# Node_b of layers 2 and 3: split in SBUF and turned by DMA instead of by PE, in newly arranged periods

## The chip, the core and the metric

The kernel runs on one core of a Trainium2 chip. The metric is the device time of one execution in microseconds, median of several runs. Engines are named as in the profile: PE (matmuls), PEld (its weight loads), DVE (VectorE), ACT (ScalarE), POOL (GpSimd), SP (SyncE, which issues all DMAs here).

## What is computed

Sixty-four graphs of 128 nodes with 384 features each pass through four blocks, each one `x = x + f(relu(layernorm(x)), adj)`. The first block has two layers (0 and 1 in the kernel), the second two (2 and 3), the third and fourth one each (4 and 5). The second block's layer, in which the changed values live, is

```
h = relu(hidden)                       # node_b, 128 nodes x 384
m_left  = h @ W_left.T                 # and m_right = h @ W_right.T
u = triu(h m_left^T) + tril(h m_right^T) ; attn = softmax of u/sqrt(384) over the edges
out = attn @ (h @ W_lin.T + b_lin) ; layer norm ; next layer
```

Blocks 3 and 4 are attention with 12 heads under the adjacency matrix; block 3 ends in an output product (Wo), block 4 does not. All large products are made from f16 halves: a value v is held as hi = f16(v) and lo = f16(v - hi), and a product takes three matmuls (hi hi, lo hi, hi lo).

## The kernel before

PE needs the node features with the features on the partitions, so each layer begins with a turning: `node` (128 nodes x 384, f32, SBUF) becomes three 128x128 blocks in a PSUM bank by three matmuls with the identity (`turned`, L420), ACT takes the high half out of the bank with Relu, and DVE the low half. For layers 2 and 3 these are `turned(b0, node_b[l])`, `htb_hi` (ACT, L721) and `htb_lo` (DVE, L871, `relu_lo`). The probabilities of layers 4 and 5 go another way: they are split in SBUF (`prob_halves`, DVE L1079 and POOL L1220) and turned by one DMA transpose for each quad of heads (`pt_halves`, SP, L315), eight a graph.

Nothing is scheduled by a compiler. On each engine the work of a graph is written as several streams (Python generators), one step for each `yield`: on PE `a` and `w` (layers 0 and 1: chain and weight products), `b` and `x` (layers 2 and 3), `c`, `y` and `t` (layers 4 and 5). `woven` runs them in periods: the string `ORDER[engine]` says letter by letter whose next step comes, `FIRST` in which period and at which occurrence a stream begins. So in one period PE works on graph g in layers 0 and 1, on an older graph in layers 2 and 3 and on a still older one in layers 4 and 5. Each engine takes its instructions strictly in this order and waits on semaphores. `SPLITS` places the splitting of the 19 weights into halves (ACT high, DVE low, one weight each time) in the first periods, and `WARM_FIRST` and `WARM_LAST` put small matmuls on ones (L626, L630) into gaps of PE in the first and last periods.

Steps that the prediction speaks of, by tile and line:

- Layer 0 and 1 on PE: turning of node_a (L420), scores, the left, right and self products (weights 0 to 5, bank_a, L374, 128x384 matmuls: a first half of four and a rest of five), turning of attn_a (L457), context product `sides` x `attn_ta`. ACT's copy L714 scales the self product by d_sum from bank a0 to a1 and so frees a0, into which attn_a is turned.
- Layers 2 and 3 on PE: left product (L406 high groups, L413 low part), right product (nine matmuls for each of three column groups, L374), score product, turning of attn_b (L505), context product lin x attn_tb.
- Layer 4 to layer 5: Wo (L374 on bank_c), `x` updated by DVE (L1119), norm (DVE stats_c, mean_var_c, var_eps_c; POOL rstd_c; DVE shift_c L1129), `node_c` by ACT (L651), its turning on PE (L420 on bank_c).
- The buffer `pt_halves` is one for both layers: the transpose of quad j of layer 4 waits until the product of quad j of layer 5 (of the older graph, L579 to L581 on bank_a) has read it.

## Time and profile before

| | us |
|---|---|
| median of 3 runs | 2900.89 (2900.38 to 2901.71) |
| the profiled execution, device time | 2899.22 |
| its span, first to last instruction | 2897.5 |
| PE busy in the span | 2794.9 |
| DVE busy | 2424.7 |
| ACT busy | 2116.5 |
| POOL busy | 846.4 |

The page of the profile gives the span, the busy time of each engine and the costliest groups of instructions. The timeline gives start and length of each instruction, in us from the start of the span, with the idle time before it and its releaser in brackets. Matmuls are pipelined, so starts are to be compared, not ends: the time that a matmul takes from PE is the distance to the start of the next.

### The profile page before, as it was taken

What the parts mean: (1) busy time and instruction counts of PE and PEld (TensorE: products, weight loads), DVE (VectorE), ACT (ScalarE), POOL (GpSimd) and SP (SyncE); (2) the same over time, 40 slices, a digit from 0 to 9 for tenths busy, and PEclk for the clock granted to TensorE, in tenths of its full rate; (3) what the DMA queues carried; (4) which work ended last, traced back from release to release, by engine and by line L of the source; (5) the groups of instructions that cost most, each with busy time, mean ns of one, the idle gap of its engine ahead of it and who ended that gap; (6) DMA issues with size and microseconds to landing.
All of it is one profiled execution on the core that took longest, in us unless ns stands there. A gap on an engine that the chain in (4) does not pass through costs nothing.

```text
span 2897.5 us, 87504 instructions
## 1 busy us (share of the span) xinstructions
PE 2794.9 (96%) x33735; PEld 2130.6 (74%) x33735; DVE 2424.7 (84%) x7450; ACT 2116.5 (73%) x6036; POOL 846.4 (29%) x1227
## 2 busy tenths in 40 slices
PE   6999999999999999999999999999999999999998
PEld 4777777777777777777777777677777777777787
DVE  5788888888888888898888888888888888888884
ACT  5677777777777777777677777777777777777763
POOL 0133233233233233233232332232332332332331
PEclk8999999999999999999999999999999999999999
DMA  6132232232232232232232322322322222322222
GB/s 220 21 56 45 50 54 45 52 53 46 52 55 44 52 54 45 52 56 43 51 49 46 55 47 49 54 46 48 57 45 49 57 47 47 57 44 49 54 50 42
DMA packets 458222, 154.85 MB, mean 53 GB/s; under 512 B 415312, under 2 KB 457808, under 8 KB 457808
## 3 DMA queue, kind: packets, MB, share of 16 engines
q1 hardware_dynamic: 457808, 149.25, 27.2%
q8 instruction: 270, 4.42, 0.6%
q14 instruction: 144, 1.18, 0.1%
HBM read 35.92 MB, written 12.58 MB: 17 GB/s over the span
## 4 chain that ended last, share of the span: by engine, by line
PE 64%; DVE 17%; DMA 8%; issue 4%; POOL 4%; SPq 2%; ACT 1%; DVEq 0%; POOLq 0%; ACTq 0%
PE bank_c L374 23%; PE bank_a L374 13%; PE bank_b L374 13%; DMA pt_halves<-prob_halves 7%; PE bank_c L548 4%; DVE score L1064 4%; PE bank_b L406 3%; POOL prob_halves L1220 2%; DVE neg_head_max L1069 2%; PE bank_c L420 2%; SPq L315 2%; PE bank_b L413 1%; DVE scaled_b L995 1%; PE bank_b L420 1%; POOL rstd_c L1171 1%
## 5 line engine op out<-in xcount | busy, mean ns | idle before, releaser
L1220 POOL TENSOR_TENSOR prob_halves<-prob,prob_halves 128x384 f16<-128x384 f32 x512 | 473.7, 930 | 597.7 <-DVE prob_halves L1079 597.6
L785 ACT ACTIVATE prob<-score,neg_head_max 128x128 f32<-128x128 f32 x1536 | 494.8, 390 | 56.5 <-DVE neg_head_max L1069 54.6
L1064 DVE SCALAR_TENSOR_TENSOR score<-bank_c,bias 128x384 f32<-128x384 f32 x512 | 281.8, 550 | 212.8 <-PE bank_c L548 202.7
L374 PE MATMUL bank_c<-htc_hi,w_lo 128*128 128x128 f16 x2304 | 405.4, 219 | 0.0
L374 PE MATMUL bank_c<-htc_lo,w_hi 128*128 128x128 f16 x2304 | 405.4, 219 | 0.0
L374 PE MATMUL bank_c<-htc_hi,w_hi 128*128 128x128 f16 x2304 | 405.4, 219 | 0.0
L374 PE MATMUL bank_a<-w_hi,hta_hi 128*128 128x384 f16 x1152 | 375.4, 326 | 0.7
L374 PE MATMUL bank_a<-w_lo,hta_hi 128*128 128x384 f16 x1152 | 375.4, 326 | 0.0
L1069 DVE TENSOR_REDUCE neg_head_max<-score 128x3 f32<-128x384 f32 x512 | 280.0, 547 | 2.4
L374 PE MATMUL bank_a<-w_hi,hta_lo 128*128 128x384 f16 x1152 | 250.3, 326 | 0.0
L374 PEld LDWEIGHTS bank_c<-htc_lo,w_hi 128*128 128x128 f16 x2304 | 225.4, 98 | 13.8
L374 PEld LDWEIGHTS bank_c<-htc_hi,w_hi 128*128 128x128 f16 x2304 | 225.9, 98 | 12.3
L646 ACT ACTIVATE bank_a<-bias_rows 128x384 f32<-128x384 f32 x384 | 189.8, 494 | 61.3 <-DVE hta_lo L871 57.2
L374 PEld LDWEIGHTS bank_c<-htc_hi,w_lo 128*128 128x128 f16 x2304 | 225.4, 98 | 0.0
L374 PE MATMUL bank_b<-htb_hi,w_lo 128*128 128x128 f16 x1152 | 202.6, 219 | 0.0
L374 PE MATMUL bank_b<-htb_lo,w_hi 128*128 128x128 f16 x1152 | 202.5, 219 | 0.0
L374 PE MATMUL bank_b<-htb_hi,w_hi 128*128 128x128 f16 x1152 | 202.4, 219 | 0.0
L646 ACT ACTIVATE m_hi<-bank_b 128x384 f16<-128x384 f32 x256 | 124.0, 485 | 105.6 <-PE bank_b L413 60.9
L374 PE MATMUL bank_a<-sides,attn_ta 128*128 128x384 f32 x512 | 195.0, 503 | 0.0
L1171 POOL TENSOR_TENSOR rstd_bc<-var_eps_bc,minus_half 128x1 f32<-128x1 f32 x64 | 35.2, 551 | 529.3 <-DVE var_eps_bc L883 529.3
L374 PE MATMUL bank_c<-w_hi,htc_hi 128*128 128x384 f16 x576 | 188.7, 328 | 0.2
L374 PE MATMUL bank_c<-w_lo,htc_hi 128*128 128x384 f16 x576 | 187.9, 327 | 0.0
(202 smaller groups left out, 8991.2 us busy)
## 6 DMA issues: line engine op xcount, KB each, us to landing
x_in<-x SPq DMA_DIRECT2D x64, 192.0 KB, 2.4
out<-y_out SPq DMA_DIRECT2D x64, 192.0 KB, 2.4
pt_halves<-prob_halves SPq DMA_TRANSPOSE x512, 2.8
w_stage<-w_t SPq DMA_DIRECT2D x11, 576.0 KB, 5.7
adj_in<-adj SPq DMA_DIRECT2D x64, 64.0 KB, 2.1
adj_t<-adj_turned SPq DMA_DIRECT2D x64, 64.0 KB, 2.2
score<-w_t SPq DMA_DIRECT2D x4, 576.0 KB, 7.3
prob<-w_t SPq DMA_DIRECT2D x4, 576.0 KB, 7.5
```

What stands on the lines that cost most here:

```text
L315: sp.dma_start_transpose(pt_halves[:, j, :, :, :].rearrange("p h c n -> p (h c) n"), prob_halves[:, j, :, :, :].rearrange("p h c n -> p (h ...
L374: mm = nc.tensor.matmul(out_ap, a, b, start=first and i == 0, stop=last and i == len(pairs_of) - 1, skip_group_check=True)
L406: nc.tensor.matmul(bank[:, cols], w[:, m, c, cols], th[:, c, :], start=(o, c, n) == (0, 0, 0), stop=False, skip_group_check=True)
L413: mm = nc.tensor.matmul(bank[:, cols], w_hi[:, m, c, cols], tl[:, c, :], start=False, stop=(o, c) == (CHUNKS - 1, CHUNKS - 1), skip_group_ ...
L420: mm = nc.tensor.matmul(bank[:, c * 128:(c + 1) * 128], src(c), ident[:, :], start=c == 0, stop=True, is_transpose=True, skip_group_check= ...
L548: mm = nc.tensor.matmul(c_banks[j][:, c * 128:(c + 1) * 128], qk[rows, c, 0, :], qk[rows, c, 1, :], start=c == 0, stop=True, skip_group_ch ...
L646: return nc.scalar.activation(dst, src, ACT.Copy, scale=scale)
L785: ex = nc.scalar.activation(prob[:, j, c, :], score[:, j, c, :], ACT.Exp, bias=neg_head_max[:, j, c:c + 1])
L1064: V.scalar_tensor_tensor(score[:, j, :, :], chunked(c_banks[j][:, 0:D]), scale, bias[:, :].unsqueeze(1).to_broadcast([128, CHUNKS, 128]), ...
L1069: V.tensor_reduce(neg_head_max[:, j, :], score[:, j, :, :], AX.X, ALU.max, negate=True)\
L1171: P.tensor_tensor(rstd[of][:, :], src, exponent[:, :], ALU.pow).then_inc(root_ready[of][g], 1)
L1220: P.tensor_tensor(prob_halves[:, j, 1, :, :], prob[:, j, :, :], prob_halves[:, j, 0, :, :], ALU.subtract)\
```

## The change

Node_b is no longer turned by PE. ACT writes the high half of node_b (Relu, f16) into `node_b_halves` in SBUF, DVE the low half beside it, and SP turns both with one DMA transpose for each layer into `htb`, whose two halves are the former `htb_hi` and `htb_lo`. The step `turned(b0, node_b...)` is gone from PE's stream `b` (8 steps a graph become 6), SP gets a new stream `b` with two steps a graph. Node_b needs one buffer instead of two. The left product waits for the landing (`htb_landed`) instead of for each half. The wait for the former reader of bank b0 moves to the right product.

All tables of the order are new: the strings of all five engines (turned round, so that a period now begins about where place 21 of PE's string was before, and with steps exchanged), FIRST, the places of the weight splits and the warming matmuls.

```diff
-    "pe": "cwyybwwbwwcbyayyyyyyyxxcxxxxxabxtxyyyybyaybyaywwtbwwwwxxaxxccxxcxcacbaxcxccaw",
+    "pe": "xxcxxxxxabtxxyyyabyybayyywwtwwwwxaxxcxxcccxxacabxxcccawcwyybwbwwcwyyyyyyyya",
...
-    "sp": "lsttttttttu",
+    "sp": "lbtttbtttttsu",
...
-    "act": [(0, -1), (0, -1), (0, -1), (0, -1), (0, -1), (0, -1), (0, -1), (0, 24),
+    "act": [(0, 5), (0, 32), (0, 42), (0, 54), (0, 59), (1, 4), (1, 21), (1, 21),
...
-        node_b = ring("node_b", 2, [128, D])
-        htb_hi, htb_lo = sb("htb_hi", [128, CHUNKS, 128], f16), sb("htb_lo", [128, CHUNKS, 128], f16)
+        node_b = sb("node_b", [128, D])
+        node_b_halves, htb = (sb(n, [128, 2, CHUNKS, 128], f16) for n in ("node_b_halves", "htb"))
+        htb_hi, htb_lo = htb[:, 0, :, :], htb[:, 1, :, :]
...
+            def turn_nodes_b(g):
+                for k in (1, 2):
+                    sp.wait_ge(*htb_lo_ready.at(g, k))
+                    if k == 1 and g:
+                        sp.wait_ge(*lin_done.at(g - 1, 2))
+                        sp.wait_ge(*ub_done.at(g - 1, 2))
+                    sp.dma_start_transpose(htb[:, :, :, :].rearrange("p h c n -> p (h c) n"),
+                                           node_b_halves[:, :, :, :].rearrange("p h c n -> p (h c n)"))\
+                        .then_inc(htb_landed[g], 16)
+                    yield
...
-                    pe.wait_ge(*node_b_ready.at(g, k))
-                    if l == 0 and g:
-                        pe.wait_ge(*scaled_b_ready.at(g - 1, 2))
-                    turned(b0, lambda c: node_b[l][:, c * 128:(c + 1) * 128]).then_inc(tb_done[g], 1)
-                    yield
...
-                    pe.wait_ge(*htb_hi_ready.at(g, k))
+                    pe.wait_ge(*htb_landed.at(g, k))
...
-                    act.wait_ge(*tb_done.at(g, k))
-                    nc.scalar.activation(htb_hi[:, :, :], chunked(b0[:, 0:D]), ACT.Relu).then_inc(htb_hi_ready[g], 1)
+                    act.wait_ge(*node_b_ready.at(g, k))
+                    if l == 0 and g:
+                        act.wait_ge(*htb_landed.at(g - 1, 2))
+                    nc.scalar.activation(node_b_halves[:, 0, :, :], chunked(node_b[:, :]), ACT.Relu).then_inc(htb_hi_ready[g], 1)
...
-                    relu_lo(htb_lo[:, :, :], b0, htb_hi[:, :, :]).then_inc(htb_lo_ready[g], 1)
+                    node_lo(node_b_halves, node_b).then_inc(htb_lo_ready[g], 1)
```

How the order moved at three places. PE in steady state, around the turning of node_c for layer 5: `w_hi,hta_hi` and `w_lo,hta_hi` on bank_a are the self product of layer 0, `w_hi,hta_lo` its low part. Before:

```order
L374 MATMUL bank_a<-w_hi,hta_hi 128x384
L374 MATMUL bank_a<-w_lo,hta_hi 128x384
L374 MATMUL bank_a<-w_hi,hta_hi 128x384
L374 MATMUL bank_a<-w_lo,hta_hi 128x384
L374 MATMUL bank_a<-w_hi,hta_hi 128x384
L374 MATMUL bank_a<-w_lo,hta_hi 128x384
L374 MATMUL bank_a<-w_hi,hta_lo 128x384 x3
L420 MATMUL bank_c<-ident,node_c 128x128 x3
L420 MATMUL bank_b<-ident,node_b 128x128 x3
```

Now:

```order
L387 MATMUL bank_a<-w_hi,hta_hi 128x384
L387 MATMUL bank_a<-w_lo,hta_hi 128x384
L387 MATMUL bank_a<-w_hi,hta_hi 128x384
L387 MATMUL bank_a<-w_lo,hta_hi 128x384
L433 MATMUL bank_c<-ident,node_c 128x128 x3
L387 MATMUL bank_a<-w_hi,hta_hi 128x384
L387 MATMUL bank_a<-w_lo,hta_hi 128x384
L387 MATMUL bank_a<-w_hi,hta_lo 128x384 x3
```

The second half of the self product stood ahead of node_c and stands behind it; node_b's turning is gone.

DVE in steady state, from the attention of layer 3 (attn_b) to shift_c, with which ACT makes node_c of layer 5. `x_1<-bank_c,x_1` is the update by Wo. Before:

```order
L985 TENSOR_SCALAR attn_b<-delta_b,r_den_b 128x128
L1119 SCALAR_TENSOR_TENSOR x_1<-bank_c,x_1 128x384
L868 SCALAR_TENSOR_TENSOR attn_tb_lo<-bank_b,attn_tb_hi 128x128
L883 TENSOR_SCALAR var_eps_ab<-squares_ab 128x1
L874 BN_STATS stats_c<-x_1 128x6
L877 BN_AGGR mean_var_c<-stats_c 128x2
L1125 TENSOR_SCALAR var_eps_c<-mean_var_c 128x1
L907 SCALAR_TENSOR_TENSOR attn_a,edge_sum<-expo_a,adj_in 128x128
L887 TENSOR_TENSOR shift_ab<-neg_mean_ab,rstd_ab 128x1
L1129 SCALAR_TENSOR_TENSOR shift_c<-mean_var_c,rstd_c 128x1
L874 BN_STATS stats_b<-bank_b 128x6
```

Now (just ahead of these rows stand attn_b and the bias of layer 5, `bias<-adj_in,beta_col,no_edge`):

```order
L921 SCALAR_TENSOR_TENSOR attn_a,edge_sum<-expo_a,adj_in 128x128
L901 TENSOR_TENSOR shift_ab<-neg_mean_ab,rstd_ab 128x1
L925 SCALAR_TENSOR_TENSOR junk_a,d_sum<-attn_a,ident 128x128
L1133 SCALAR_TENSOR_TENSOR x_1<-bank_c,x_1 128x384
L878 SCALAR_TENSOR_TENSOR attn_tb_lo<-bank_b,attn_tb_hi 128x128
L888 BN_STATS stats_c<-x_1 128x6
L928 SCALAR_TENSOR_TENSOR den_a<-z_sum,edge_sum 128x1
L891 BN_AGGR mean_var_c<-stats_c 128x2
L1139 TENSOR_SCALAR var_eps_c<-mean_var_c 128x1
L888 BN_STATS stats_b<-bank_b 128x6
L891 BN_AGGR mean_var_b<-stats_b 128x2
L1143 SCALAR_TENSOR_TENSOR shift_c<-mean_var_c,rstd_c 128x1
```

The bias, attn_a, shift_ab and junk_a moved ahead of the update of x, and stats_b with its aggregate between var_eps_c and shift_c.

ACT at the start of the program: `w_hi` rows are weight splits, `spent_in` belongs to the input's norm of graph 0. Before:

```order
L848 ACTIVATE w_hi<-w_stage 128x1152 x2
L848 ACTIVATE w_hi<-score 128x1152
L848 ACTIVATE w_hi<-prob 128x1152
L848 ACTIVATE w_hi<-w_stage 128x1152 x2
L848 ACTIVATE w_hi<-score 128x1152
L656 ACTIVATE spent_in,total_in<-x_in 128x384
L646 ACTIVATE neg_mean_in<-total_in 128x1
L662 ACTIVATE spent_in,squares_in<-x_in,neg_mean_in 128x384
L848 ACTIVATE w_hi<-prob 128x1152
L848 ACTIVATE w_hi<-w_stage 128x1152
L651 ACTIVATE node_a<-x_in,shift_in,rstd_in 128x384
```

Now:

```order
L664 ACTIVATE spent_in,total_in<-x_in 128x384
L858 ACTIVATE w_hi<-w_stage 128x1152
L654 ACTIVATE neg_mean_in<-total_in 128x1
L670 ACTIVATE spent_in,squares_in<-x_in,neg_mean_in 128x384
L858 ACTIVATE w_hi<-w_stage 128x1152
L659 ACTIVATE node_a<-x_in,shift_in,rstd_in 128x384
L858 ACTIVATE w_hi<-score 128x1152
L703 ACTIVATE hta_hi<-bank_a 128x384
```

Two weight splits instead of nine stand ahead of node_a of graph 0. One more pair of rows moved on PE without a table here: the turning of attn_a of layer 1 (L457) stood behind twelve high matmuls of layer 3's left product and stands now behind six of them.

## Rows read from the trace of the kernel before

**Rows 1.** The page, part 1: busy us (share), instructions.
```profile
PE 2794.9 (96%) x33735; PEld 2130.6 (74%) x33735; DVE 2424.7 (84%) x7450; ACT 2116.5 (73%) x6036; POOL 846.4 (29%) x1227
```

**Rows 2.** Windows by stage: from:to us, then busy by engine, clock, DMA share, GB/s.
```profile
0.00:30.00 30.00, 8.83 (x118) 8.66 (x118) 12.16 (x18) 13.55 (x16) 2.39 (x12) 0.71 0.94 333
30.00:62.30 32.30, 27.49 (x269) 20.40 (x269) 20.09 (x42) 20.10 (x37) 1.65 (x3) 0.95 0.46 155
...
171.10:2783.90 2612.80, 2550.80 (x30600) 1934.27 (x30599) 2241.26 (x6959) 1957.53 (x5633) 790.88 (x1139) 1.00 0.27 50
2783.90:2897.50 113.60, 101.12 (x1592) 87.98 (x1590) 66.87 (x171) 49.61 (x141) 24.86 (x32) 0.97 0.28 44
```

**Rows 3.** Timeline of PE around two turnings: start us, us, instruction [idle before].
```profile
1202.35 0.55 PE L420 MATMUL bank_b<-ident,node_b 128*128 128x128 f32 x3
1202.73 0.33 PE L374 MATMUL bank_a<-w_hi,hta_hi 128*128 128x384 f16 x1
...
1223.77 0.55 PE L420 MATMUL bank_c<-ident,node_c 128*128 128x128 f32 x3
1224.48 0.52 PE L420 MATMUL bank_b<-ident,node_b 128*128 128x128 f32 x3 [0.17 <-DVE scaled_b L995]
...
1224.90 0.34 PE L374 MATMUL bank_c<-w_hi,htc_hi 128*128 128x384 f16 x1
```

**Rows 4.** Waits of PE: total us, times, longest us.
```profile
PE bank_c L579 <- DMA pt_halves<-prob_halves: 47.9, 58, 2.4
```

**Rows 5.** Timeline of PE: product of quad 0, layer 5, then layer 4.
```profile
1207.60 0.18 PE L579 MATMUL bank_a<-v_hi,pt_halves 128*128 128x33 f16 x1
...
1212.41 0.19 PE L579 MATMUL bank_c<-v_hi,pt_halves 128*128 128x33 f16 x1 [0.85 <-DMA pt_halves<-prob_halves]
```

**Rows 6.** Tile pt_halves: issue to landing of 512 transposes.
```profile
DMA to landing us min/median/max: 2.7/2.8/5.3
```

**Rows 7.** Timeline of PE: turning of attn_b, right behind Wo.
```profile
1220.20 0.27 PE L505 MATMUL bank_b<-ident,attn_b 128*128 128x128 f32 x1
```

**Rows 8.** Chain of waits, 1217 to 1226: start us, us, piece.
```profile
1220.40 0.56 DVE x L1119
...
1222.17 0.56 POOL rstd_c L1171
...
1222.75 0.16 DVE shift_c L1129
1222.91 0.48 DVE stats_b L874
```

**Rows 9.** The page, part 4: the chain by engine.
```profile
PE 64%; DVE 17%; DMA 8%; issue 4%; POOL 4%; SPq 2%; ACT 1%; DVEq 0%; POOLq 0%; ACTq 0%
```

**Rows 10.** Timeline of ACT: node_c of layer 5.
```profile
1223.01 0.71 ACT L651 ACTIVATE node_c<-x,shift_c,rstd_c 128x384 f32<-128x384 f32 x1
```

**Rows 11.** Timeline of DVE: node_b's steps and the ones moved.
```profile
1204.02 0.55 DVE L871 SCALAR_TENSOR_TENSOR htb_lo<-bank_b,htb_hi 128x384 f16<-128x384 f32 x1
...
1222.02 0.29 DVE L907 SCALAR_TENSOR_TENSOR attn_a<-expo_a,adj_in 128x128 f32<-128x128 f32 x1
...
1223.31 0.28 DVE L911 SCALAR_TENSOR_TENSOR junk_a<-attn_a,ident 128x128 f32<-128x128 f32 x1
...
1242.85 0.56 DVE L874 BATCH_NORM_STATS2 stats_b<-bank_b 128x6 f32<-128x384 f32 x1
...
1244.83 0.72 DVE L1008 SCALAR_TENSOR_TENSOR node_b<-scaled_b,inv_sd,norms 128x384 f32<-128x384 f32 x1
```

**Rows 12.** Timeline of PE and ACT: turning of attn_a, layer 1.
```profile
1205.65 0.22 PE L406 MATMUL bank_b<-htb_hi,w_hi 128*128 128x128 f16 x1
1205.95 0.53 ACT L714 ACTIVATE bank_a<-bank_a,d_sum 128x384 f32<-128x384 f32 x1
1206.62 0.30 PE L457 MATMUL bank_a<-ident,attn_a 128*128 128x128 f32 x1
```

**Rows 13.** Timeline of ACT and DVE at the start.
```profile
28.45 1.16 ACT L848 ACTIVATE w_hi<-w_stage 128x1152 f16<-128x1152 f32 x1 [0.33 <-DMA w_stage<-w_t]
29.52 0.69 ACT L651 ACTIVATE node_a<-x_in,shift_in,rstd_in 128x384 f32<-128x384 f32 x1
49.96 0.47 ACT L695 ACTIVATE hta_hi<-bank_a 128x384 f16<-128x384 f32 x1
62.32 0.55 DVE L951 SCALAR_TENSOR_TENSOR x<-scaled_a,x_in 128x384 f32<-128x384 f32 x1
```

More of the change, by code:

```diff
@@ L22 @@
 ORDER = {
-    "pe": "cwyybwwbwwcbyayyyyyyyxxcxxxxxabxtxyyyybyaybyaywwtbwwwwxxaxxccxxcxcacbaxcxccaw",
-    "act": "gwenwmicnwbjccjccjnbcbfjcgkbxccbakeknakeewebcwcwccqbbfagexipbaeieib",
-    "dve": "bbpbipppaipbabbbabcjbcacccjbccbjhaccnabhaqbkacbabaxnbhhakbbabbbaacaccbcchcchaczhhzbbpaazaa"
-           "apaaipbabxp",
-    "pool": "bmbhmnqahhbhhhhhaac",
-    "sp": "lsttttttttu",
+    "pe": "xxcxxxxxabtxxyyyabyybayyywwtwwwwxaxxcxxcccxxacabxxcccawcwyybwbwwcwyyyyyyyya",
+    "act": "ibnemgcnwnjjjcwcccbjbcfgckcqbxcbankekaekebwecwwcccbbgfaxeiiibpaeewb",
+    "dve": "apbpappbbpbbbbcjnjcjancccbccbccahcabkabaababhxbahbbabbbkbaahaccccchccaahczhhzbpbapzaaabaai"
+           "pbaxbipbqai",
+    "pool": "nmmhahhbhqhhhhaacbb",
+    "sp": "lbtttbtttttsu",
 }
 FIRST = {
[5 rows of a table removed]
[5 rows of a table added]
 }
 SPLITS = {
-    "act": [(0, -1), (0, -1), (0, -1), (0, -1), (0, -1), (0, -1), (0, -1), (0, 24),
-            (0, 27), (0, 45), (0, 46), (0, 48), (0, 59), (1, 8), (1, 16), (1, 18),
-            (1, 27), (1, 45), (2, 22)],
-    "dve": [(0, -1), (0, -1), (0, -1), (0, -1), (0, -1), (0, -1), (0, 4), (0, 72),
-            (0, 78), (0, 78), (0, 100), (1, 13), (1, 21), (1, 26), (1, 68), (1, 68),
-            (1, 68), (2, 16), (2, 65)],
-    "sp": [(0, -1), (0, -1), (0, -1), (0, 9), (0, 10), (1, 5), (1, 5), (1, 7),
-            (1, 7), (2, 10), (3, 5)],
+    "act": [(0, 5), (0, 32), (0, 42), (0, 54), (0, 59), (1, 4), (1, 21), (1, 21),
+            (1, 29), (1, 46), (1, 46), (2, 13), (2, 17), (2, 48), (2, 48), (2, 49),
+            (3, 17), (3, 43), (3, 62)],
+    "dve": [(0, -1), (0, 44), (0, 98), (0, 100), (0, 100), (1, 1), (1, 24), (1, 66),
+            (1, 66), (1, 75), (2, 16), (2, 24), (2, 24), (2, 75), (3, 16), (3, 16),
+            (3, 83), (3, 100), (4, 16)],
+    "sp": [(0, -1), (0, -1), (0, 2), (0, 4), (0, 12), (2, 1), (2, 5), (2, 5),
+            (2, 5), (3, 12), (4, 0)],
 }
@@ L198, in gnn_stack_kernel @@
         x1_ready = Signal("x1_ready")
-        node_b_ready, tb_done = Signal("node_b_ready", 2), Signal("tb_done", 2)
+        node_b_ready, htb_landed = Signal("node_b_ready", 2), Signal("htb_landed", 2, 16)
         adj_t_loaded = Signal("adj_t_loaded", 1, 16)
@@ L526, in weight_b @@
                     weights(g, 2 + l, 1)
-                    pe.wait_ge(*htb_lo_ready.at(g, k))
+                    if l == 0 and g:
+                        pe.wait_ge(*scaled_b_ready.at(g - 1, 2))
                     for o in range(CHUNKS):
@@ L675, in start_b @@
                 if g:
-                    act.wait_ge(*tb_done.at(g - 1, 1))
-                scale("ab", g, node_b[0], x1[g % 2], node_b_ready)
+                    act.wait_ge(*htb_lo_ready.at(g - 1, 2))
+                scale("ab", g, node_b, x1[g % 2], node_b_ready)
                 yield
@@ L719, in chain_b @@
                     k = l + 1
-                    act.wait_ge(*tb_done.at(g, k))
-                    nc.scalar.activation(htb_hi[:, :, :], chunked(b0[:, 0:D]), ACT.Relu).then_inc(htb_hi_ready[g], 1)
+                    act.wait_ge(*node_b_ready.at(g, k))
+                    if l == 0 and g:
+                        act.wait_ge(*htb_landed.at(g - 1, 2))
+                    nc.scalar.activation(node_b_halves[:, 0, :, :], chunked(node_b[:, :]), ACT.Relu).then_inc(htb_hi_ready[g], 1)
                     yield
@@ L868, in lo_part, with node_lo @@
                 return V.scalar_tensor_tensor(dst, src, scale, hi, op0=ALU.mult, op1=ALU.subtract)
+            def node_lo(halves, node):
+                return V.scalar_tensor_tensor(halves[:, 1, :, :], chunked(node[:, :]), 0.0, halves[:, 0, :, :],
+                                              op0=ALU.max, op1=ALU.subtract)
             def relu_lo(dst, bank, hi):
@@ L1005, in chain_b @@
                     dve.wait_ge(*scaled_b_ready.at(g, k))
-                    dst = (node_b[1], scaled_b)[l]
+                    dst = (node_b, scaled_b)[l]
                     done = (node_b_ready, affine_b_ready)[l]
```

5 lines of the change are left out of this document (1 added, 4 removed), and 21 rows, old and new, of tables (FIRST, WARM_FIRST, WARM_LAST).

## The prediction

> **What bounds the kernel now.** I read the page's busy shares first: PE is busy for 2794.9 us of 2897.5 us [rows 1]. The windows by stage say where: in the 2612.8 us in which 60 graphs pass in steady state, PE is busy for 2550.8 us, 97.6%, at clock 1.00; DVE is next with 2241.3 us, 86%. In the first 62.3 us PE works for 36.3 us only [rows 2]. One period is 2612.8 / 60 = 43.5 us. So two kinds of thing move the time: what PE executes or waits for in a period (times 64), and the start and the end. The chain of waits agrees, and shows one place in each period where it leaves PE for DVE, POOL and ACT: from the update of x with layer 4's output product to the turning of node_c for layer 5 [rows 8, 9]. That place decides below. The profiled execution took 2899.22 us, 1.7 us less than the median; I sum differences against it and apply them to the median.
>
> **Turnings of node_b off PE.** One turning (three 128x128 f32 matmuls) starts at 1202.35, the work after it at 1202.73; the other takes from 1224.48 to 1224.90: 0.80 us of PE a graph. The one of layer 2 also waited: the turning of node_c before it starts at 1223.77 and would have made way after 0.38 us, but node_b starts at 1224.48, so 0.33 us of idle goes too [rows 3]. That is 1.13 us a graph, 64 graphs: **-72 us**. ACT's high and DVE's low half of node_b stay one operation each of 384 columns, now read from SBUF instead of PSUM; the nearest row is the present one (0.55 us on DVE [rows 11]), and I take no difference.
>
> **Wait for the turned probabilities.** PE waits 47.9 us for pt_halves in 58 waits [rows 4]. The cause is a buffer: the transpose of quad 0 of layer 4 is issued only when layer 5's product has read that quad of pt_halves, at 1207.60 + 0.4 us, and PE comes to the new data at 1212.41 after 0.85 us of idle [rows 5]. So PE has 3.5 us of other work in between, against landings of 2.7 to 5.3 us, median 2.8 [rows 6]: each wait is a late landing. In the new order the low part of layer 3's left product (nine 128x128 matmuls at 0.056 us) and one more quad's product (0.24 us) come in between, and PE has 4.2 us. 0.7 us more slack takes at most 0.7 us from each of 58 waits of 0.83 us mean: 0 to -40 us. They are uneven (the longest is 2.4 us), so a good half: **-26 us**.
>
> **The new wait, which decides.** Before, the chain from layer 4's output product to node_c starts when PE has finished that product and turns attn_b, at 1220.20 [rows 7]; it ends when ACT's node_c (1223.01 + 0.71 = 1223.72) lets PE turn it at 1223.77 [rows 3, 10]: 3.57 us, with 0.05 us to spare. PE filled that with the right product of layer 0, a context product and the whole self product. The new order of PE puts the second half of the self product (0.81 us) behind the turning of node_c. PE then has 2.76 us of work for a chain of 3.5 us: 0.76 us of wait even if nothing else moved. But DVE's order changes too. Ahead of the update of x now stand bias3, attn_a, shift_ab and junk_a, which stood elsewhere: 0.24 + 0.29 + 0.07 + 0.28 = 0.9 us (bias3 taken like attn_a's shape [rows 11], shift_ab a single column). DVE had 0.33 us to spare there, between attn_b's end and 1220.40 [rows 8], and tri_u (0.34 us) now stands before all this: the update comes 0.2 to 0.3 us late. Between var_eps_c and shift_c now stand stats_b and its aggregate, 0.5 + 0.2 us, beside POOL's 0.56 us [rows 8]: 0.2 us late again. The chain becomes 3.8 to 4.0 us and the wait 1.1 us. Part of it will show earlier, at layer 3's context product, since attn_tb_lo stands behind the same update. 64 times: **+70 us**, bounds 0.76 us (+49) and 1.4 us (+90).
>
> **Turning of attn_a in layer 1.** It waits for ACT's copy that frees bank_a. Before, 0.97 us pass from the end of the self product (1205.65) to the turning (1206.62): twelve matmuls of layer 3 fill 0.66 us, 0.3 us is idle; ACT's copy runs 1205.95 to 1206.48 [rows 12]. Now six of the twelve stand behind the turning, so the idle grows by 0.33 us: **+21 us**, and nothing hides it.
>
> **The transposes themselves.** Layer 3's is the tight one. Before, stats_b starts at 1242.85 and node_b is written at 1244.83 + 0.72 [rows 11]: 2.7 us. Then the high half (0.5), the low half (0.55), semaphores (0.2) and 2.8 us to landing, of the same shape on the same queue [rows 6]: 6.75 us, about 7.0 from the end of the context product's issue. In its new order PE has there one score product of layer 1, three groups of layer 4's K, six halves of layer 1's side products and layer 4's scores: 0.5 + 1.5 + 4.4 + 0.9 = 7.3 us. The first matmuls on htb also stand just ahead of the turning of attn_a, which waits 0.64 us anyway, so a landing in up to 3.7 us is free. SP issues this transpose between quads 2 and 3 of layer 5, and quad 3 is read only 3 us after the htb matmuls start. Layer 2's has about 2 us to spare. I take **+2 us**, bounds 0 and +25. Beside the rows: the Trainium skill, page "VectorE: DVE Perf Modes", section "The three transpose paths", gives 390 ns on TensorE against 1309 ns by DMA for one 128x128 block and advises TensorE where PSUM will do. Six blocks in a row would be 7.9 us by that figure, an estimate, 4.2 us beyond the slack, and the sum about 270 us higher. This trace disagrees: 512 transposes of six blocks landed in 2.8 us at the median. I give that reading a chance of 0.01.
>
> **The start.** Before, ACT's first seven weight splits stand ahead of graph 0: node_a comes at 29.52, the second hta_hi at 49.96, x1 of graph 0 at 62.32; the ninth weight is split at 28.45, as it lands [rows 13]. Now two splits stand ahead of node_a and nine ahead of the second hta_hi, which can come at about 33 us, since the weights land as before; x1 of graph 0 with it, 17 us earlier. Some is given back: about eight ACT splits (1.16 us) and nine of DVE move into periods 2 to 4, where one or two wait for a weight in flight. **-12 us**, bounds -18 and -2. The last stage (113.6 us [rows 2]) keeps its make-up: no term.
>
> **Sum**: -72 - 26 + 70 + 21 + 2 - 12 = -17 us, so 2900.9 - 17 = **2884 us**.
>
> **Rivals.** (1) The moved DVE work hides, the chain stays at 3.5 us and most late landings are covered: -72 - 36 + 49 + 21 + 0 - 15 = -53, 2845 to 2868 us. For it: DVE idles for 14% of the steady stage [rows 2]. Against: in this stretch it works back to back. Chance 0.27. (2) Slower: layer 3's transpose lands late in every period, because it shares SP's queue and the DMA engines with eight others. It costs from a landing of 3.7 us on, where layer 3's slack ends, and with the other terms as summed the kernel is slower from about 4.0 us: at 4.5 us 0.8 us a graph, +51 - 2, 2933 us; at 5.3 us 2984 us. For it: such landings exist [rows 6]. Against: the median. Chance 0.13. (3) It does what it says and comes out even: the chain costs 1.4 us (+20) or the start gives back what it wins (+10): 2894 to 2908 us. Chance 0.17. The forecast, 2869 to 2893 us, has 0.42, and 0.01 is the page's.
>
> **How the numbers follow.** A measurement of this kernel tells about 0.2%, 5.8 us, from no change. Faster by more: the forecast and rival 1, 0.69. Same: most of rival 3, 0.14. Slower: rival 2, the page's reading and the rest of rival 3, 0.17. All cheap bounds together give 2900.9 - 60 = 2841 us, all dear ones 2900.9 + 62 = 2963. With one tenth left out on each side the range is 2850 to 2918 us.
>
> **What would show it.** Right: no turning of node_b on PE; idle of PE before node_c's turning or layer 3's context product near 1.1 us a graph; idle before one turning of attn_a near 0.6 us a graph; waits for pt_halves near 20 us; hardly any for htb; x1 of graph 0 near 45 us; a period near 43.4 us. Wrong: idle before the first matmuls on htb in most periods (rival 2), node_c turned without idle and a period near 42.8 us (rival 1), or x1 of graph 3 no earlier than before.

## The result, and the profile after

The changed kernel takes **2867.41 us** (median of 4 runs, 2863.91 to 2869.98) against 2901.3 us of the kernel before beside it (2900.38 to 2901.8): ratio 0.9882, 95% interval 0.9869 to 0.9895. That is 34 us faster. A second set of runs gave 2866.23 us beside 2898.95 us of the kernel before, ratio 0.9886 (0.9871 to 0.9902). One execution of a later kernel (experiment 10) took 7029.59 us, for which nothing on record gives a cause; it is left out of every comparison. The prediction was 2884 us, faster.

The page of the changed kernel, part 1 (to be held against [rows 1]), then its windows (as [rows 2]: busy us by engine, clock, DMA share, GB/s) to graph 0's x1, the first norm's update of x, then over 60 graphs and at the end:

```profile
PE 2762.5 (96%) x33523; PEld 2095.5 (73%) x33523; DVE 2437.3 (85%) x7450; ACT 2115.4 (74%) x6036; POOL 847.0 (30%) x1227
```
```profile
0.00:30.00 30.00, 24.05 (x258) 19.53 (x259) 14.27 (x33) 17.02 (x30) 3.49 (x14) 0.94 0.93 313
30.00:43.60 13.60, 11.62 (x109) 8.00 (x108) 8.45 (x19) 8.33 (x15) 0.55 (x1) 1.00 0.68 227
161.50:2754.00 2592.50, 2511.45 (x30232) 1891.17 (x30229) 2254.00 (x6958) 1956.35 (x5633) 790.45 (x1139) 1.00 0.33 60
2754.00:2868.30 114.30, 103.72 (x1673) 92.67 (x1670) 66.61 (x171) 50.59 (x142) 25.69 (x33) 0.98 0.28 47
```

The span went from 2897.5 to 2868.3 us, by 29.2 us: 9.6 us until x1 of graph 3 (161.5 for 171.1), 20.3 us in the 60 periods that follow (2592.5 for 2612.8), and the end gave back 0.7. The profiled execution is the slowest of its four, so this trace shows 29.2 of the 34 us. A mean period is 43.2 us for 43.5.

The waits of PE in the changed kernel (us in total, times, longest us; the first is the wait of [rows 4]):

```profile
PE bank_c L587 <- DMA pt_halves<-prob_halves: 32.4, 41, 1.7
PE bank_a L470 <- ACT bank_a L722: 23.1, 58, 0.5
PE bank_a L387 <- ACT bank_a L654: 21.4, 63, 3.0
PE bank_b L419 <- DMA htb<-node_b_halves: 7.7, 9, 1.5
```

The timeline of PE from the turning of attn_b behind Wo (as [rows 7]) to the first product of V (as the last of [rows 3]); the first column is the start in us:

```profile
1244.67 0.27 PE L513 MATMUL bank_b<-ident,attn_b 128*128 128x128 f32 x1
...
1245.68 0.34 PE L387 MATMUL bank_b<-lin_hi,attn_tb_hi 128*128 128x384 f16 x1
...
1247.43 0.32 PE L387 MATMUL bank_a<-w_hi,hta_hi 128*128 128x384 f16 x1 [0.28 <-ACT bank_a L654]
...
1248.18 0.55 PE L433 MATMUL bank_c<-ident,node_c 128*128 128x128 f32 x3
...
1249.38 0.33 PE L387 MATMUL bank_c<-w_hi,htc_hi 128*128 128x384 f16 x1
```

And the timelines of DVE and ACT on the same way (as [rows 8, 10, 11]):

```profile
1244.64 0.29 DVE L925 SCALAR_TENSOR_TENSOR junk_a<-attn_a,ident 128x128 f32<-128x128 f32 x1
...
1244.87 0.56 DVE L1133 SCALAR_TENSOR_TENSOR x<-bank_c,x 128x384 f32<-128x384 f32 x1
...
1247.16 0.16 DVE L1143 SCALAR_TENSOR_TENSOR shift_c<-mean_var_c,rstd_c 128x1 f32<-128x1 f32 x1
...
1247.42 0.71 ACT L659 ACTIVATE node_c<-x,shift_c,rstd_c 128x384 f32<-128x384 f32 x1
```

What to see: from the turning of attn_b (1244.67) to that of node_c (1248.18) are 3.51 us, against 3.57 before. The x update still starts 0.20 us behind the turning of attn_b, although bias3, attn_a, shift_ab and junk_a now stand ahead of it on DVE.

**Where the 20.3 us of the steady stage went.** I took, over the 60 periods of both timelines, every start of a PE group that comes more than 0.06 us later than the pace of the group before allows (from start to start 0.056 us for a 128x128 f16 matmul, 0.163 for 128x384, and so on), and summed by the group that was late. This counts the 0.1 to 0.2 us that the waits view leaves out. How much is put down to a group depends by some us on the pace that is taken, above all ahead of node_b's turnings.

| 60 periods, us | before | after | difference | forecast for 60 |
|---|---|---|---|---|
| PE's own work (the rest) | 2492.8 | 2449.6 | -43.2 | -48 |
| ahead of node_b's turnings | 22.8 | 0 | -22.8 | -20 |
| ahead of products on pt_halves | 52.5 | 38.2 | -14.3 | -24 |
| layer 3's context, self product, node_c, V | 6.2 | 48.4 | +42.2 | +66 |
| ahead of the turnings of attn_a | 17.9 | 31.1 | +13.2 | +20 |
| ahead of the first matmuls on htb | 0.1 | 5.1 | +5.0 | +2 |
| ahead of the scores and head_out's turning | 19.5 | 19.8 | +0.3 | 0 |
| sum | 2612.8 | 2592.5 | -20.3 | -4 |

Small entries (1.1 us before, 0.4 after) are left out. In the shortest periods, which no late landing disturbs, it is plainer still: 42.60 us before, 42.57 after. PE's idleness in them went from 1.1 to 1.7 us, nearly as much as its work went down by.

### The profile page after: what moved, and what is told of

It reads as the page before. It is cut to its first block, busy times and chain, and to the rows that moved or that the text cites. A ratio compares the mean times of both kernels' runs of the same rounds, so it can differ in the third digit from the quotient of the medians.

```text
span 2868.3 us, 87271 instructions
## 1 busy us (share of the span) xinstructions
PE 2762.5 (96%) x33523; PEld 2095.5 (73%) x33523; DVE 2437.3 (85%) x7450; ACT 2115.4 (74%) x6036; POOL 847.0 (30%) x1227
## 4 chain that ended last, share of the span: by engine, by line
PE 70%; DMA 8%; DVE 8%; ACT 6%; issue 4%; POOL 2%; SPq 1%; ACTq 0%; DVEq 0%; POOLq 0%
PE bank_c L387 22%; PE bank_a L387 18%; PE bank_b L387 14%; DMA pt_halves<-prob_halves 6%; PE bank_c L556 4%; PE bank_b L419 3%; DVE score L1078 3%; PE bank_c L433 3%; POOL prob_halves L1234 2%; DVE neg_head_max L1083 2%; PE bank_b L426 1%; ACT node_b L659 1%; SPq L317 1%; DVE prob_halves L1093 1%; ACT node_b_halves L731 1%
## 5 line engine op out<-in xcount | busy, mean ns | idle before, releaser
L387 PE MATMUL bank_c<-htc_hi,w_hi 128*128 128x128 f16 x2304 | 399.0, 219 | 0.0
L387 PE MATMUL bank_c<-htc_lo,w_hi 128*128 128x128 f16 x2304 | 399.0, 219 | 0.0
L387 PE MATMUL bank_c<-htc_hi,w_lo 128*128 128x128 f16 x2304 | 399.0, 219 | 0.0
L387 PE MATMUL bank_b<-htb,w_hi 128*128 128x128 f16 x2304 | 213.1, 219 | 0.0
L387 PE MATMUL bank_b<-w_hi,htb 128*128 128x384 f16 x768 | 208.1, 326 | 0.0
L387 PE MATMUL bank_b<-htb,w_lo 128*128 128x128 f16 x1152 | 202.6, 219 | 0.0
L387 PEld LDWEIGHTS bank_a<-w_hi,hta_hi 128*128 128x128 f16 x1152 | 112.3, 97 | 101.2 <-issue 40.7
```

Of the source, the lines that this page charges most:

```text
L387: mm = nc.tensor.matmul(out_ap, a, b, start=first and i == 0, stop=last and i == len(pairs_of) - 1, skip_group_check=True)
```

## Experiments

All edits are to the changed kernel unless it is said otherwise. Where ORDER is edited, a letter is one step of a stream, and places are counted from 0. No run has the new order with node_b still turned by PE, so what the new order would be worth without the transposes is open.

**1. The transpose without the rearrangement.** The periods of before, without PE's two places for the turnings; SP's two steps b are put in.

```diff
 ORDER["pe"], of before: two letters b (places 11 and 49) taken out
-    "sp": "lsttttttttu",
+    "sp": "lsbttttbttttu",
```

The places of the warming matmuls and of SP's weight loads are counted anew with it; the orders of ACT, DVE and POOL are those of before.

> One part alone: node_b of layers 2 and 3 is split into halves and turned by the DMA transpose as in the changed kernel, but the periods of before stay, only without the two places of the turnings on PE. In before's trace layer 3's first column product starts 3.3 us behind the turning of node_b and layer 2's 5.0 us; the way by two copies (0.6 us each, one after the other) and a landing of 2.8 us is about 4.2 us behind node_b. Theory A (the rearrangement is what makes the transpose hide): PE waits for htb 1 to 2 us in every graph, most of it in layer 3, and the 1.14 us a graph that the turnings cost is lost again: 2900 to 3000 us, likeliest 2950. Rival B (the turnings alone carry the gain, the rearrangement nothing): 2850 to 2885 us.

Measured: 3043.93 us, ratio 1.0498 (1.0484 to 1.0512): 145 us slower than before. The waits of PE:

```profile
PE bank_b L453 <- DMA htb<-node_b_halves: 148.2, 78, 4.3
PE bank_c L621 <- DMA pt_halves<-prob_halves: 41.5, 50, 1.7
PE bank_c L421 <- ACT htc_hi L789: 36.3, 62, 0.8
```

Theory A holds in kind, but the time lies above its range, 94 us above its likeliest value. Three things had not been in it. First the way from node_b to the landing: theory A had 4.2 us. From the end of node_b, layer 3's transposes landed after 5.6 us at the median and layer 2's after 5.2, against 3.9 us for layer 3 in the changed kernel. SP was not late: it issued within 0.03 us of DVE's low half. In the old orders ACT begins the high half 0.8 to 1.0 us behind node_b, and DVE the low half 0.9 to 1.5 us behind that (changed kernel, layer 3: 0.03 and 0.56 us). So 1.6 us of layer 3's lateness lie in where the two halves stand on ACT and DVE. Second, the third row: with the turning of node_b gone from behind that of node_c, V comes up to 0.8 us early, and waits for ACT's htc_hi. Part of what a turning cost had been covering another wait. The third is the clock. A timeline row of PE, and the windows around it (as [rows 2]):

```profile
1321.74 0.23 PE L453 MATMUL bank_b<-htb,w_hi 128*128 128x128 f16 x1 [1.94 <-DMA htb<-node_b_halves]
```
```profile
1317.00:1320.00 3.00, 2.80 (x18) 1.47 (x15) 3.00 (x8) 2.34 (x7) 0.00 (x0) 1.00 0.33 62
1320.00:1323.00 3.00, 1.26 (x16) 1.20 (x17) 1.33 (x5) 1.74 (x6) 1.82 (x2) 0.88 0.35 66
1323.00:1326.00 3.00, 3.00 (x47) 3.00 (x45) 3.00 (x6) 1.56 (x5) 0.93 (x1) 0.55 0.01 3
1326.00:1329.00 3.00, 3.00 (x50) 2.37 (x48) 1.85 (x7) 0.98 (x2) 0.93 (x2) 1.00 1.02 116
```

Behind 1.94 us of idleness the granted clock falls to 0.55, that is mostly the lower of its two levels (1.2 for 2.4 GHz), for some 3 us. It does not do so each time: of the 63 idle times above 1.5 us between 190 and 2900 us, 21 have such a stretch at or behind them, and others of the same length have none. Over the run the clock was 0.982, against 0.996 in the kernel before: 0.014 x 3044 = 43 us at most, an estimate.

**2. The start alone.** The kernel before, with the splits and loads of the weights placed in ACT's, DVE's and SP's first periods much as in the changed kernel.

```diff
 SPLITS, of before
-    "act": [(0, -1), (0, -1), (0, -1), (0, -1), (0, -1), (0, -1), (0, -1), (0, 24),
+    "act": [(0, 5), (0, 24), (0, 45), (0, 54), (0, 59), (1, 3), (1, 20), (1, 20),
...
-    "dve": [(0, -1), (0, -1), (0, -1), (0, -1), (0, -1), (0, -1), (0, 4), (0, 72),
+    "dve": [(0, -1), (0, 52), (0, 100), (1, 9), (1, 9), (1, 13), (1, 28), (1, 70),
...
```

> Before, with nothing changed but where the weights' splits and their loads stand in the first periods of ACT, DVE and SP: 2 of ACT's copies ahead of node_a of graph 0 instead of 9, and 1 or 2 on DVE instead of 7, as in the changed kernel. Theory A (the start's gain of 18.7 us at graph 0 is half given back by the third graph, 9.6 us stay): x1 of graph 0 near 45 us instead of 62.3, ratio about 0.996 (2888 to 2894 us). Rival B (all of it is given back, since the later splits then stand in the way of graphs 1 to 3): 2898 to 2904 us, no change.

Measured: 2888.05 us, 0.9962 (0.9949 to 0.9974), 10.9 us faster than before. x1 of graph 0 (first row) and of graph 3 (last), to be held against 62.32 [rows 13]:

```profile
42.50 0.55 DVE L946 SCALAR_TENSOR_TENSOR x<-scaled_a,x_in 128x384 f32<-128x384 f32 x1
...
159.16 0.55 DVE L946 SCALAR_TENSOR_TENSOR x<-scaled_a,x_in 128x384 f32<-128x384 f32 x1
```

19.8 us are won at graph 0, 12 are left at graph 3, 10.9 at the end. Theory A holds. So about a third of the change's 34 us has nothing to do with the transpose.

**3. Taking the wait ahead of attn_a's turning.** From here on the second set of the changed kernel (after_again) is what the runs are held against.

```diff
 ORDER["pe"], places 32 to 35
-    xaxx
+    xxxa
```

> The changed kernel unaltered, as the yardstick beside the other runs of this chip: 2864 to 2870 us by both theories; if it lies elsewhere, the other runs are to be read against this one.

> The changed kernel with one letter of PE's period moved: the turning of attn_a of layer 1 stands behind all three high products of layer 3 instead of behind the first. It waits for ACT's copy of the self product, which ends 1.0 us behind that product's end; 0.33 us of work stands between now and 0.56 us of idleness, 0.99 us of work would stand between. Theory A (this idleness is on the path like any other of PE): idle before the turning of attn_a near 0 (23 us in all now), 20 to 36 us less than the changed kernel: 2832 to 2848 us. Rival B (the time goes into waits for htb or for pt_halves that follow, since those landings do not move): 2860 to 2870 us.

Measured: changed kernel 2866.23 us; this one 2884.3 us, 0.9948 (0.9935 to 0.9962), slower than the changed kernel by 18 us. Its waits of PE:

```profile
PE bank_a L587 <- DVE attn_ta L932: 31.7, 61, 0.5
PE bank_a L387 <- ACT bank_a L654: 21.9, 62, 3.3
PE bank_b L419 <- DMA htb<-node_b_halves: 14.1, 16, 2.4
```

The wait for L722 is gone and one for DVE's attn_ta stands in its place: the first product of layer 5's probabilities uses the same bank and may start only when DVE has read the turned attn_a. And the waits for htb doubled (6.2 us in after_again). The 10 us more at the first place and the 8 us more at the second make up the 18 us. Before this edit a late htb was free up to 0.5 us, because PE would have waited right behind it at attn_a anyway: periods with 1.0 us ahead of htb show no idleness at attn_a. Both theories missed: the gain did not only pass on, it turned into a loss. The loss is one of the disturbed periods: the shortest is 42.61 us for 42.57.

**4. Both sides of that wait.**

```diff
 ORDER["pe"], places 32 to 41
-    xaxxcxxccc
+    xxxaxcxccc
```

> As ata_later (the turning of attn_a of layer 1 behind the three high products), and the first probability product of layer 5 one place later as well, behind the low products of layer 3. In ata_later the 22 us before the turning went, but 31.7 us came before that probability product, which waits for DVE's copy attn_ta of the same bank: it needs 0.65 us behind the turning, and only 0.35 us of work stood between. Now 0.50 us plus the turning's own 0.13 stand between. Theory A (the two waits are one chain, self product to ACT copy to turning to DVE copy to probability product, and it fits once both sides are moved): both waits near 0, probability product at its old absolute time, 15 to 32 us less than the changed kernel, 2834 to 2852 us. Rival B (what is gained there is given back by later waits for htb, pt_halves or the chain behind Wo): 2860 to 2885 us.

Measured: 2890.33 us, 0.9964 (0.9951 to 0.9976), 24 us slower than the changed kernel. Rival B in kind, 5 us beyond its range. In its shortest period, 42.60 us, the 0.56 us ahead of attn_a are gone and PE idles 0.2 to 0.35 us ahead of node_a's turning, 0.18 ahead of the probability product and 0.14 ahead of layer 3's scores product. One of them on PE's timeline:

```profile
933.15 0.52 PE L433 MATMUL bank_a<-ident,node_a 128*128 128x128 f32 x3 [0.21 <-DVE head_out L1124]
```

They are work of ACT and DVE behind the same self product: ACT copies it, then takes nine exponentials and m_hi, and DVE's m_lo and head_out follow. PE arriving earlier only waits later. That explains why nothing was won; the loss again lies in the periods with late landings. The waits for htb were 13.0 us for 6.2, and those for pt_halves 49.2 us for 37.9, most of them here:

```profile
PE bank_c L587 <- DMA pt_halves<-prob_halves: 45.7, 51, 1.8
```

**5. The wait behind Wo: is it ACT, or the way to node_c?**

```diff
 ORDER["act"], places 0 to 7; the first weight split goes from (0, 5) to (0, 7)
-    ibnemgcn
+    ibemgcnn
```

> The changed kernel with ACT's row copy of the self product's bias and the scaling of node_c ahead of the two passes over x of graph g (0.7 us), so that ACT is free for both. PE now stands idle 0.28 us before the self product (released by that bias copy) and 0.10 before the turning of node_c. Theory A (the way from Wo over the x update, its statistics and shift_c to node_c is the limit; shift_c ends 0.10 us before node_c starts): the idle time only moves to the turning of node_c, 0 to 8 us less than the changed kernel: 2858 to 2868 us. Rival B (ACT is the limit there): the 0.38 us a graph go, 18 to 24 us less: 2840 to 2850 us.

Measured: 2879.82 us, 0.9935 (0.9922 to 0.9947), 12 to 14 us slower than the changed kernel. The waits of PE at the place:

```profile
PE bank_c L428 <- ACT node_c L654: 23.0, 64, 0.4
```

The wait for the bias copy (20.2 us in after_again) fell to 3.1, and all of it came up at node_c. In both kernels the turning of node_c starts 3.30 us behind the x update, to 0.01 us. Theory A is right on the mechanism: the way from Wo over x, its statistics and shift_c is the limit. It is wrong on the total, since the two passes over x_in were not free behind V either: the scores of layer 5 came 0.20 us later (10.06 for 9.86 us behind the x update).

**6. The self product's second half.**

```diff
 ORDER["pe"], places 64 and 65
-    cw
+    wc
```

> The changed kernel with the second half of the self product of layer 0 (0.81 us) ahead of the turning of node_c instead of behind it, as PE had it before. Theory A (the work is only taken from one wait and given to the other, since V of layer 5 needs htc_hi 1.0 to 1.1 us behind the start of that turning): the wait before the turning goes down to 0, the wait for htc_hi before V comes up at 0.6 to 0.7 us a graph, as in turn_only (36.3 us, 62 times): within 0.5% of the changed kernel either way, 2855 to 2885 us, likeliest 2868. Rival B (the wait before the turning is the only one): 0.5 us a graph less, about 2838 us.

Measured: 2905.2 us, 1.0018 (1.0008 to 1.0028): 39 us slower than the changed kernel, worse than theory A's range.

```profile
PE bank_c L387 <- ACT htc_hi L755: 37.5, 64, 0.8
```

The wait at V came up as forecast (0.75 us a graph by the timeline's pace). What theory A got wrong is the other side: the 0.81 us of work had only 0.10 us of idleness to fill there, and the turning of node_c came 0.72 us later behind the x update. The changed kernel's place is right: that half product belongs where the copy htc_hi has to be waited for.

**7. SP's queue.**

```diff
-    "sp": "lbtttbtttttsu",
+    "sp": "lbttttbttttsu",
```
(the three weight loads that stood at SP's place 5 of period 2 stand at place 6)

> The changed kernel with SP's transpose of node_b of layer 3 one place later, behind the fourth quad of probabilities instead of ahead of it. In the changed kernel it is issued at 1226.13 and its product starts at 1229.53; the fourth quad is issued at 1227.94. Theory A (SP works its queue in order, and an issue holds it 1.21 us): the issue comes at about 1229.15, landing at 1232, PE waits 2 to 2.5 us for htb in every graph, and as in turn_only the granted clock falls behind a wait of that length: 130 to 260 us slower than the changed kernel, 3000 to 3130 us. Rival B (the queue's order costs little because the fourth quad is ready early): under 40 us slower.

Measured: 3029.63 us, 1.0442 (1.0426 to 1.0459).

```profile
PE bank_b L414 <- DMA htb<-node_b_halves: 156.3, 64, 3.7
```

Theory A holds: 2.4 us in each of the 64 graphs, and a granted clock of 0.977. Layer 3's transpose was now issued 3.09 us behind DVE's low half, for 0.03. One place in SP's queue is worth 163 us here.

**8. Is DVE the bound?** In the changed kernel's shortest period DVE has no gap above 0.12 us from the first score of layer 5 to the variance of the next x2, some 37 us. Two kernels shorten its work.

```diff
-                    V.tensor_reduce(head_min[:, quads, :], score[:, quads, :, :], AX.X, ALU.min)
+                    V.tensor_reduce(head_min[:, quads, :], score[:, quads, :, 0:16], AX.X, ALU.min)
```

> The changed kernel with the two head_min reductions of layer 4 on DVE taken over 16 of the 128 columns instead of all (0.95 us each becomes about 0.2), so the test for rows without an edge sees only those columns. Observed so far: the shortest period is 42.57 us in the changed kernel, 42.61 in ata_later and 42.60 in ata_and_pv, although these took 0.56 us of idleness off PE; and in such a period DVE has no gap between the first score of layer 5 and var_eps_bc, some 37 us. Theory A (DVE's run without a gap from the score of layer 5 to head_out of layer 4, and then PE's way over Wo, node_c, V, q and k to the scores, is a loop that sets the shortest period; DVE is as much the bound as PE): the shortest period falls below 42.57, here only by 0.1 to 0.2 us since PE keeps its other waits, and since the last quad of probabilities comes 0.75 us earlier the waits for pt_halves fall from 38 us to 10 to 25; 18 to 45 us less than the changed kernel, 2822 to 2850 us. Rival B (PE alone is the bound, the waits for pt_halves come from slow landings whatever DVE does): within 6 us of the changed kernel.

> ata_and_pv with the same shortened head_min reductions. ata_and_pv lost 16 to 24 us against the changed kernel instead of gaining. Theory A (there PE had become ready before DVE, so its gain was not to be had): with DVE's run 1.5 us shorter the move of the turning of attn_a pays: the shortest period falls by 0.4 to 0.7 us below 42.57, and this kernel is 10 to 35 us faster than min_short. Rival B (the move of that turning costs by itself, by the waits for htb that grew from 6 to 13 us): still 10 to 25 us slower than min_short.

Measured: min_short 2871.34 us, 0.9898 (0.9884 to 0.9913); min_short_ata 2890.65 us, 0.996 (0.9948 to 0.9972). No gain in either: min_short lies within 6 us of the changed kernel (its rival B), and min_short_ata 19 us above min_short (its rival B), with 58.0 us of waits for pt_halves and 17.6 for htb. But this does not show that DVE is no bound, since hardly any of the shortening was gained. DVE's groups in min_short (busy us, mean ns | idle before):

```profile
L1101 DVE TENSOR_REDUCE head_min<-score 128x6 f32<-128x96 f32 x128 | 30.9, 241 | 0.0
L1093 DVE CAST prob_halves<-prob 128x384 f16<-128x384 f32 x512 | 238.0, 465 | 19.4 <-ACT prob L795 19.4
```

and the cast in the changed kernel:

```profile
L1093 DVE CAST prob_halves<-prob 128x384 f16<-128x384 f32 x512 | 177.5, 356 | 0.1
```

head_min went from 120.9 us to 30.9, 90 us less. The casts, which nothing had touched, took 60.5 us more, and DVE waited 19.4 us for ACT, which leaves 10 us in 64 graphs. The timelines of DVE and GpSimd show why:

```profile
887.26 0.92 POOL L1234 TENSOR_TENSOR prob_halves<-prob,prob_halves 128x384 f16<-128x384 f32 x1 [0.30 <-DVE prob_halves L1093]
```
```profile
886.51 0.67 DVE L1093 CAST prob_halves<-prob 128x384 f16<-128x384 f32 x1
887.49 0.91 DVE L1093 CAST prob_halves<-prob 128x384 f16<-128x384 f32 x1 [0.30 <-ACT prob L795]
```

The second cast starts while GpSimd's operation on the quad before runs (887.26 to 888.18), and ends at 888.40, 0.22 us behind it, as if it had begun only then; alone it takes 0.35. In the changed kernel a head_min reduction stands at that place, and is not stretched. This is so throughout: in min_short 134 of the 512 casts begin while an operation of GpSimd on prob_halves runs, and every one ends 0.21 to 0.33 us behind it; the other 378 take 0.34 to 0.36 us. The Trainium skill, page "SBUF — State Buffer", section "Who interferes with whom", says that a cast on DVE can run in a mode that takes the port pair it shares with GpSimd, that whoever comes second blocks for the whole instruction, and that a reduction never contends. The traces agree with it: the casts end behind GpSimd's operation, and the 62 reductions neg_head_max that begin beside one take 0.55 us as the others do. That it is this port pair no row shows; the rows show the times.

**9. Earlier probabilities.**

```diff
 ORDER["dve"], places 72 to 76
-    czhhz
+    chzhz
```

> The changed kernel with one step of DVE's period moved: the cast of the third quad of probabilities of layer 4 stands ahead of the first head_min reduction (0.95 us) instead of behind it. ACT has that quad ready 0.2 us behind the place where it now stands (883.8 to 883.64), so DVE would idle 0.2 us and the third and fourth quads reach GpSimd and SP's queue 0.6 us earlier. Theory A (the waits for pt_halves are what is left when a landing of 2.7 to 5.3 us meets the slack between the last issue and its product, 1.6 us in the median now): the waits fall from 38 us to 20 to 28, the shortest period grows by 0.0 to 0.2 us, together 0 to 18 us less than the changed kernel: 2850 to 2868 us. Rival B (nothing on DVE may idle, the 0.2 us a graph count in full and the waits stay): 10 to 15 us slower, about 2880 us.

Measured: 2871.87 us, 0.99 (0.9887 to 0.9912), 6 us slower than the changed kernel, between the two theories. Two of its waits of PE:

```profile
PE bank_a L432 <- DVE head_out L1123: 13.7, 47, 0.3
PE bank_c L586 <- DMA pt_halves<-prob_halves: 11.0, 18, 1.3
```

The waits for pt_halves fell to 15 us (with 3.9 of the other bank), further than theory A had it: they do hang on the slack between issue and use. The step moves the last two quads, and it is ahead of layer 4's last quad that the waits went, from 26.5 us to 4.1, while those ahead of quad 0 stayed (7.3 and 7.0). The mean period stayed, 43.23 for 43.21 us, since the short periods became longer: 37 of 60 lie within 0.06 us of 43.10, such as this one (starts of two neighbouring x1, and the same two of the changed kernel's second set, 42.57 us apart):

```profile
852.52 0.55 DVE L964 SCALAR_TENSOR_TENSOR x<-scaled_a,x_in 128x384 f32<-128x384 f32 x1
895.65 0.55 DVE L964 SCALAR_TENSOR_TENSOR x<-scaled_a,x_in 128x384 f32<-128x384 f32 x1
```
```profile
848.16 0.55 DVE L965 SCALAR_TENSOR_TENSOR x<-scaled_a,x_in 128x384 f32<-128x384 f32 x1
890.73 0.55 DVE L965 SCALAR_TENSOR_TENSOR x<-scaled_a,x_in 128x384 f32<-128x384 f32 x1
```

The 0.54 us are mostly the same stretching. GpSimd runs from 628.82 to 629.74, and on DVE's timeline:

```profile
628.38 0.36 DVE L1092 CAST prob_halves<-prob 128x384 f16<-128x384 f32 x1
628.65 0.55 DVE L1082 TENSOR_REDUCE neg_head_max<-score 128x3 f32<-128x384 f32 x1
629.25 0.70 DVE L1092 CAST prob_halves<-prob 128x384 f16<-128x384 f32 x1
```

The moved cast now lies beside GpSimd's operation and takes 0.70 us for 0.35, the next 0.43; with some 0.1 us of waiting for ACT that is 0.5. Over the run the casts took 209.7 us for 177.4. So 0.5 us a graph paid for what the earlier probabilities won.

**10. The same, with head_out put right.**

```diff
 ORDER["dve"], places 72 to 79
-    czhhzbpb
+    chzhbpbz
```

> phi_first with a second step of DVE's period moved: the second head_min reduction (0.95 us) behind the two low parts of m and head_out of layer 5 instead of ahead of them. In phi_first the waits for pt_halves fell from 38 to 15 us, and yet the time stayed, since every period grew from 42.57 to 43.12 us: the turning of node_a of layer 0 stood idle 0.45 us behind head_out, and the product behind m_lo 0.13. Theory A (the two new waits are that reduction's 0.87 us ahead of m_lo and head_out, and go when it stands behind them, while the earlier probabilities stay): the shortest period returns to 42.5 to 42.7 us, the waits for pt_halves stay near 15 to 22 us, 15 to 30 us less than the changed kernel, 2836 to 2852 us. Rival B (what is taken from one wait comes back at another, as in ata_later, ata_and_pv, bias_first and phi_first: the chain over ACT's copies and head_out is a limit of its own): the shortest period 42.9 us or more, 2862 to 2880 us.

Measured: 2878.95 us, 0.9931 (0.9918 to 0.9944), 13 us slower than the changed kernel. The wait for head_out went, the shortest period stayed:

```profile
853.21 0.55 DVE L964 SCALAR_TENSOR_TENSOR x<-scaled_a,x_in 128x384 f32<-128x384 f32 x1
896.33 0.55 DVE L964 SCALAR_TENSOR_TENSOR x<-scaled_a,x_in 128x384 f32<-128x384 f32 x1
```

That is 43.12 us. In its place PE idles 0.27 us more ahead of the self product and 0.3 us at u of layer 0 or at pt_halves. Rival B holds: two orders of DVE with the same stretched casts have the same shortest period to 0.01 us, wherever PE waits in it. What made this kernel 7 us slower than the one of experiment 9 is another thing: PE comes to layer 4's last quad earlier again (1.7 us behind the end of SP's issue at the median, for 2.2 in experiment 9), and the waits for pt_halves rose from 15 to 33 us.

```profile
PE bank_c L586 <- DMA pt_halves<-prob_halves: 29.4, 43, 1.5
```

So once DVE loses half a microsecond, its run without a gap does seem to set the period; in the changed kernel itself it lies level with the way over PE, ACT and head_out (min_short: 42.49 us, 0.08 less). That the two are level is inferred from these periods; no run took away both at once.

No variant beat the changed kernel.

## Why the prediction was right, and where it was short

The direction, the range (2850 to 2918 us) and most signs held. Two signs did not: PE waits 36 us for pt_halves, not 20, and the new wait is 0.8 us a graph, not 1.1. Of this only 0.1 us stands ahead of node_c's turning, 0.25 stand ahead of layer 3's context product and over 0.4 ahead of the self product. The result lies 17 us below the forecast, just outside the band of the forecast proper (2869 to 2893) and at the upper end of rival 1's (2845 to 2868), whose own signs, no idleness ahead of node_c and a period near 42.8 us, did not come either. In part the closeness is luck: in the table the new wait came out 24 us below its term and the turning of attn_a 7, and the waits for pt_halves 10 above theirs. Step by step:

- **Turnings of node_b off PE, -72 us.** In 60 periods -43.2 and -22.8, -66 us, where the step has -68. Right. But the order was changed with it: experiment 1 took the same turnings out of the old order, and V waited 36 us for htc_hi.
- **Wait for pt_halves, -26.** The waits of PE come to 50.3 us before and 36.3 after, -14. The mechanism, slack against late landings, is right by experiment 9; the size is half. The step read the slack of quad 0 and gave it to all 58 waits. But of the 48 us before, 33 stood ahead of layer 4's last quad and 14 ahead of quad 0; after, it is 24 and 8. For the last quad the median time from the end of SP's issue to PE's coming grew from 1.5 to 1.7 us only.
- **The new wait, +70: the mis-sized term.** It measured +42 for 60 periods, 0.80 us a graph less 0.1 us that V no longer waits. The step's lower bound, 0.76, was the value. What failed is the reading that the update of x comes 0.2 to 0.3 us late because bias3, attn_a, shift_ab and junk_a stand ahead of it, and shift_c 0.2 late again: x starts 0.20 us behind the turning of attn_b as before, and shift_c 2.29 us behind x for 2.35. Before, DVE stood idle 0.34 us ahead of x in the shortest period; now it begins attn_b 0.4 us earlier (0.82 for 0.42 us ahead of the turning of attn_b), and has worked the four off just when Wo's product is ready; stats_b fits beside POOL's 0.56 us. Experiment 5 shows the rest of the step right: the way Wo to node_c is the limit, at 3.5 us, and the self product's wait is only the same wait seen earlier. That is rival 1's chain, with the forecast's other terms.
- **Turning of attn_a, +21.** 0.29 became 0.56 us, +13 in 60 periods. Right in kind; a late htb in front of it hides a part. "Nothing hides it" was too strong, and experiments 3 and 4 show that this idleness costs nothing by itself: taken away, it comes back three steps on.
- **The transposes, +2.** 128 of them landed in 2.7 to 5.0 us, median 2.8, and PE waited 7.7 us in 9 cases. Rival 2's mechanism exists, and experiments 1 and 7 show its price, but the places on ACT, DVE and SP keep it rare. The reading by the time that the Trainium skill, page "VectorE: DVE Perf Modes", section "The three transpose paths", gives for one block (270 us more) is excluded: the issue of six blocks takes 1.21 us and the landing 2.8.
- **The start, -12.** -9.6 in the trace, -10.9 by itself in experiment 2. Right; x1 of graph 0 came at 43.65, forecast near 45.

The landing times of the transposes by tile htb in the changed kernel (min, median, max):

```profile
DMA to landing us min/median/max: 2.7/2.8/5.0
```

## What to carry to other kernels

Where an in-order engine waits at several places in a period, its idle times cannot be added up as gains: each has to be followed to the next thing that would be late, and a wait right behind a DMA may be what makes a late landing harmless. An operation taken off the bound engine may be worth its time only if the work around it, on every engine, is placed anew; here the DMA transposes with their new order and start are worth -34 us (11 of them by the start alone), and in the old order +145 us. When extra work is put on an engine ahead of a critical step, look at when the producer before it now ends, before charging the extra work.
